# Cross-attention: the last of 257 keys is taken off all the others

## The reference

```python
q = hidden_states @ Wq
k = encoder_hidden_states @ Wk
v = encoder_hidden_states @ Wv
scores = einsum('bhsd,bhkd->bhsk', q, k) * scale
probs = softmax(scores, axis=-1)
out = einsum('bhsk,bhkd->bhsd', probs, v)      # then @ Wo + bo
```

## Time and profile before

| what | before |
|---|---|
| median of 3 runs | 1652.82 us (1651.26 to 1653.18) |
| profiled execution, its own time | 1654.9 us |
| its span, first to last instruction | 1653.0 us |
| mean granted TensorE clock | 0.988 |
| TensorE busy | 1592.7 us |
| VectorE / ScalarE / GpSimd busy | 1112.3 / 771.1 / 240.4 us |

### The profile page before, as it was taken

How to read it: one execution, slowest core, us unless ns; L and a number is a source line. 1 busy time by engine, 2 the same in 40 slices (tenths; PEclk the granted TensorE clock), 3 DMA queues, 4 the chain that set the end, 5 groups by cost and what they waited for, 6 DMA issues and landing times.

```text
span 1653.0 us, 33814 instructions
## 1 busy us (share of the span) xinstructions
PE 1592.7 (96%) x12498; PEld 1324.8 (80%) x12498; DVE 1112.3 (67%) x2350; ACT 771.1 (47%) x1683; POOL 240.4 (15%) x153
## 2 busy tenths in 40 slices
PE   7999879999999999999999999999999999997989
PEld 6888668899989899898998898787878778775444
DVE  7776666677566766676566766657656665566788
ACT  4555554565555554555555553433123222222755
POOL 0000123232222223232222222100000000000000
PEclk9999989999999999999999999999999999998999
DMA  6898842331333213331323123250221311323022
GB/s 230 322 358 341 315 164 106 117 126 33 114 117 117 79 67 117 117 117 40 116 110 125 61 84 109 78 186 27 83 78 33 109 47 39 114 101 156 0 102 102
DMA packets 70812, 200.76 MB, mean 121 GB/s; under 512 B 4752, under 2 KB 22608, under 8 KB 67920
## 3 DMA queue, kind: packets, MB, share of 16 engines
q1 hardware_dynamic: 70736, 199.68, 32.6%
HBM read 129.28 MB, written 70.39 MB: 121 GB/s over the span
## 4 chain that ended last, share of the span: by engine, by line
PE 83%; issue 6%; DVE 6%; DMA 3%; ACT 1%; SPq 0%; POOLq 0%; POOL 0%; DVEq 0%
PE psum_o L672 16%; PE psum_s L641 12%; PE psum_o L1350 6%; PE psum_q L1350 5%; PE psum_o L687 5%; PE psum_q L700 5%; PE psum_o L533 5%; PE psum_q L1390 4%; PE psum_q L641 4%; PE psum_t L1418 4%; PE psum_t L652 3%; PE psum_t L612 2%; PE psum_s L1404 2%; PE psum_q L659 2%; PE psum_s L1377 1%
## 5 line engine op out<-in xcount | busy, mean ns | idle before, releaser
L672 PE MATMUL psum_o<-pT,c_nat 128*128 128x512 f32 x1152 | 311.6, 407 | 4.7 <-issue 3.5
L641 PE MATMUL psum_s<-cT,qk 128*128 128x258 f32 x1728 | 254.1, 291 | 10.0 <-ACT probs L861 5.3
L641 PEld LDWEIGHTS psum_s<-cT,qk 128*128 128x128 f32 x1728 | 227.0, 191 | 21.4 <-issue 6.2
L672 PEld LDWEIGHTS psum_o<-pT,c_nat 128*128 128x128 f32 x1152 | 205.1, 191 | 41.3 <-DVE pT L926 4.5
L1208 POOL TENSOR_TENSOR c_nat<-c_raw,zero 128x768 fp32r<-128x768 f32 x64 | 95.3, 1490 | 799.7 <-PE psum_o L672 603.4
L861 ACT ACTIVATE probs<-psum_s,nmax 128x257 f32<-128x257 f32 x192 | 91.7, 478 | 222.9 <-DVE nmax L1112 222.7
L1096 DVE SCALAR_TENSOR_TENSOR oT<-p_last,c_last,psum_o 128x512 f32<-128x512 f32 x192 | 143.2, 746 | 69.8 <-PE psum_o L672 67.5
L926 DVE TENSOR_TENSOR pT<-psum_t,pT 128x512 fp32r<-128x512 f32 x128 | 87.8, 687 | 73.1 <-ACT pT L752 73.1
L1211 POOL TENSOR_TENSOR c_nat<-c_raw,c_nat 128x768 fp32r<-128x768 f32 x64 | 122.3, 1911 | 5.0
L752 ACT ACTIVATE cT<-psum_t 128x256 fp32r<-128x256 f32 x192 | 67.5, 389 | 113.8 <-PE psum_t L612 113.8
L1112 DVE TENSOR_REDUCE nmax<-psum_s 128x1 f32<-128x257 f32 x192 | 81.0, 422 | 50.4 <-PE psum_s L641 49.6
(11 more groups left out here) (268 smaller groups left out, 3022.8 us busy)
## 6 DMA issues: line engine op xcount, KB each, us to landing
qk_by_tile<-staged SPq DMA_DIRECT2D x32, 1536.0 KB, 9.9
raw<-qk_by_tile SPq DMA_DIRECT2D x16, 3072.0 KB, 9.9
c_raw<-in_ctx_dram SPq DMA_DIRECT2D x64, 384.0 KB, 3.2
out_dram<-x_out SPq DMA_DIRECT2D x32, 256.0 KB, 2.1
x_res<-in_x_dram SPq DMA_DIRECT2D x16, 256.0 KB, 2.7
x_in<-out_dram SPq DMA_DIRECT2D x4, 1024.0 KB, 7.9
x_res<-out_dram SPq DMA_DIRECT2D x16, 256.0 KB, 2.8
x_all<-out_dram SPq DMA_DIRECT2D x1, 4096.0 KB, 13.2
```

The lines of the kernel that those rows point to most:

```text
L641: m = pe.matmul(ps[:, 0:SKP], qk[:, part, rg, c, b, :], cT[b % 2][:, moving, c, :], start=(c, part, moving) == (0, 0, 0), stop=(c, part) = ...
L672: i = pe.matmul(ps[:], c_nat[(b - 1) % 2][:, part, k, m * P:(m + 1) * P], pT[:, moving, k, :], start=(k, part, moving) == (0, 0, 0), stop= ...
```

## The change

Softmax doesn't change when one number is added to all scores of a row. So GpSimd now subtracts the last context row from the other 256 (`c_raw` in place, `pool_less_last`). The 257th score is then always zero, and since the probabilities sum to one, the attended result only lacks the last context row itself. What follows in the code:

- `pe_probs_last`, `act_probs_last` and `act_last_key` go; `cT`'s column 256 is zeroed once for each buffer. The scores are still 258 columns wide. The scalings cover 256 columns in place of 257.
- `dve_attended` becomes one addition of a column (`c_last`) to what it reads from PSUM. `c_last` comes from `rem_all`, unsplit.
- The context's high part goes from GpSimd to ScalarE (`act_ctx_high`), in its list between the probabilities' high parts and the next `qk` piece or exp 1. It waits for the subtraction of the same batch. GpSimd's low part waits for it.
- GpSimd's list in turn `b` is: low part of batch `b`, then the subtraction for batch `b+1` (in the "first" section one for batch 0 stands ahead).
- `pe_ctxT` waits for that subtraction (`s_sub`) in place of the load.
- Each context load is followed by a second one, which spreads the last row over 128 partitions (`last_row`, 1536 bytes each).
- Scores 3 use bank q1 in place of s0.

```diff
@@ pe_ctxT
             if chunks[0] == 0:
-                pe.wait_ge(s_ctx[(b + 1) % 2], 32 * t + 16 * ((b + 1) // 2 + 1))
+                pe.wait_ge(s_sub, 4 * t + (b + 2))
@@ pe_cross_tile
                 pe_scores(pe, t, b, 2, section)
-                if before:
-                    pe_probs_last(pe, t, b, section)
@@ ScalarE
+        def act_ctx_high(act, t, b, section):
+            i = b % 2
...
+            act.wait_ge(s_sub, 4 * t + (b + 1))
+            nc.scalar.activation(flat(c_nat[i][:, 0, :, :]), flat(c_raw[i][:]), ACT.Copy).then_inc(s_chi, 1)
@@ act_cross_tile
                 if before:
                     for k in range(2):
                         act_probsT(act, t, b, k, section)
+                act_ctx_high(act, t, b, section)
                 if b == 3 and more:
                     act_qk_high(act, t + 1, 0)
                 exp(b, 1)
...
-                if before:
-                    act_probs_last(act, t, b, section)
...
-                    act_last_key(act, b + 1, 4 * t)
@@ dve_attended
-            nc.vector.scalar_tensor_tensor(oT[:, m, :, (b - 1) % 4, :], p_last[:].rearrange("p (s q) -> p s q", q=SQ),
-                                           c_last[:, (b - 1) % 2, m:m + 1], ps[:].rearrange("p (s q) -> p s q", q=SQ),
-                                           ALU.mult, ALU.add).then_inc(free, 1)
+            nc.vector.tensor_scalar(oT[:, m, :, (b - 1) % 4, :], ps[:].rearrange("p (s q) -> p s q", q=SQ),
+                                    c_last[:, (b - 1) % 2, m:m + 1], None, ALU.add).then_inc(free, 1)
@@ GpSimd
+        def pool_less_last(pool, t, b):
+            i = b % 2
+            pool.wait_ge(s_ctx[i], 64 * t + 32 * (b // 2 + 1))
+            row_ = last_row[i][:].rearrange("p (a d) -> p a d", a=1).to_broadcast([P, 2, DC])
+            nc.gpsimd.tensor_tensor(c_raw[i][:], c_raw[i][:], row_, ALU.subtract).then_inc(s_sub, 1)
@@ pool_split
-            G.tensor_tensor(flat(c_nat[i][:, 0, :, :]), flat(c_raw[i][:]), zero[:].to_broadcast([P, 2 * DC]),
-                            ALU.add).then_inc(s_chi, 1)
             pool.wait_ge(s_chi, 4 * t + (b + 1))
             G.tensor_tensor(c_nat[i][:, 1, :, :], c_raw[i][:], c_nat[i][:, 0, :, :].bitcast(F32),
                             ALU.subtract).then_inc(s_nat, 1)
@@ pool_cross_tile
+            if section == "first":
+                pool_less_last(pool, t, 0)
             for b in range(4):
                 pool_split(pool, t, b, section)
+                if section != "last" or b < 3:
+                    pool_less_last(pool, t, b + 1)
@@ load_ctx
+            last = keys[:, 2 * P:SK, :].rearrange("a k d -> (a k) d").to_broadcast([P, DC])
+            sp.dma_start(last_row[ahead % 2][:], last).then_inc(s_ctx[ahead % 2], 16)
```

More of the change, by code:

```diff
@@ L68, in cross_units @@
     for b in range(4):
-        u += [(("S", b, rg), ("s0", "s1", "q0", "s0")[rg]) for rg in range(4)]
+        u += [(("S", b, rg), ("s0", "s1", "q0", "q1")[rg]) for rg in range(4)]
         if b or section != "first":
@@ L87, in split_only @@
 def split_only(units):
-    return [u for u in units if u[0][0] in ("XT", "Q", "WK", "RT", "CT", "PT", "W")]
+    return [u for u in units if u[0][0] in ("XT", "Q", "WK", "CT", "PT", "W")]
 def split_only2(units):
@@ L278, in build_kernel @@
         c_raw0 = sb("c_raw0", [P, 2, DC], F32)
[L279 to L284, removed]
+        rem_all = nc.alloc_sbuf_tensor_at("rem_all", [P, KC, NB], F32, offset=X_BUFS + 2 * DC * 4)
+        last_row = [sb(f"last_row{i}", [P, DC], F32) for i in range(2)]
         c_raw1 = nc.alloc_sbuf_tensor_at("c_raw1", [P, 2, DC], F32, offset=X_BUFS)
@@ L630, in pe_scores @@
         def pe_scores(pe, t, b, rg, section):
-            if rg == 0:
-                pe.wait_ge(s_key, 4 * t + (b + 1))
+            if section == "first" and rg == 0 and b < 2:
+                pe.wait_ge(s_zero, b + 1)
             if b == 0:
@@ L653, in pe_probsT @@
                 m.then_inc(done, 1)
[L655 to L661, removed]
         def pe_pv(pe, t, b, m, section):
@@ L787, in act_start_weights @@
             if r:
-                act_high(act, project(("RT",)), flat(remT[:, 0, :, :]), cols(KC * NB))
+                ps, free = full(act, project(("RT",)))
+                nc.scalar.activation(flat(rem_all[:]), ps[:, 0:KC * NB], ACT.Copy).then_inc(free, 1)
         def act_qk_high(act, t, rg):
@@ L794, in act_qk_high, with act_last_scalars @@
                                  raw[:, :, rg, :].rearrange("p h (a q) -> p h a q", q=SQ), ACT.Copy).then_inc(s_qhi, 1)
[L796 to L804, removed]
+        def act_last_scalars(act, t, b, section):
+            if section == "first" and b == 0:
+                taken(act, project(("RT",)))
+            elif b == 0:
+                act.wait_ge(drained["o1"], U1.before("o1", t, section, 1))
+            elif section != "first" or b > 1:
+                taken(act, U1(("PV", b - 1, 2), t, section))
+            batch = 4 * t
+            later = rem_all[:, :, b:]
             one = later[:, :, batch:batch + 1] if isinstance(batch, int) else later[:, :, bass.ds(batch, 1)]
@@ L825, in act_project_all @@
                 else:
-                    act_last_key(act, 0, 0)
                     for c in range(KC):
@@ L838, in act_wo_high @@
             nc.scalar.activation(wo_high[:, 4 * h:4 * h + 4, :], wo_raw[:, 4 * h:4 * h + 4, :], ACT.Copy).then_inc(s_wohi, 1)
[L840 to L847, removed]
+        def act_ctx_high(act, t, b, section):
+            i = b % 2
+            if b > 1 or (b == 1 and section != "first"):
+                full(act, U1(("PV", b - 1, 2), t, section))
+            elif b == 1:
+                full(act, U1(("CT", 0, 2), t, section))
+            elif section == "first":
+                full(act, project(("CT", "start", 2)))
+            else:
+                act.wait_ge(filled["o1"], U1.before("o1", t, section))
+            act.wait_ge(s_sub, 4 * t + (b + 1))
+            nc.scalar.activation(flat(c_nat[i][:, 0, :, :]), flat(c_raw[i][:]), ACT.Copy).then_inc(s_chi, 1)
         def act_probsT(act, t, b, k, section):
@@ L893, in act_cross_tile @@
                 if after:
-                    act_last_key(act, b + 1, 4 * t)
                     ctxT(b, 0)
                     ctxT(b, 1)
-                if section == "first" and b == 0:
-                    act.wait_ge(s_remsum, 1)
-                act_last_scalars(act, b, 4 * t)
+                act_last_scalars(act, t, b, section)
                 if b == 3 and not more:
```

37 lines of the change are left out of this document (12 added, 25 removed).

## The result

| | before | changed |
|---|---|---|
| median | 1652.72 us | 1691.26 us (1691.20 to 1691.82, 4 runs) |
| ratio | | 1.0237, 95% interval 1.0224 to 1.0249 |
| profiled execution / its span | 1654.9 / 1653.0 us | 1691.8 / 1690.0 us |
| mean granted clock | 0.988 | 0.987 |

The account below looks back on a forecast made before the run. TensorE, busy 100.00 of 100 us in the loop, was taken to bound the kernel. Loop tiles (14 x 2.48 = 34.7) and edges (+4.0) added 38.7 to 1654.9, so 1693.6 profiled, 1691 us median; range 1672 to 1708.

Parts of the forecast that it names:

- TensorE saves 0.44 a turn: Every batch: the four turnings of the 257th probability leave TensorE, 0.44 us each time, 28.2 us over 64 batches.
- The chain delivers 1.20 late: Batches 1 and 3: TensorE waits 1.20 us for GpSimd's subtraction ahead of the context's turning, +0.76 a turn.
- The fourth batch: Fourth batch of a tile: VectorE's `qk` low part comes 1.57 us late, so the turn grows by 1.4 us.
- The sum: Whole kernel: 14 loop tiles of +2.48 give 34.7, with edges of +4.0 38.7; profiled 1693.6, median 1691 us.
- The first tile: First tile: subtraction (2.0) behind a late context load, some 2 us of queued loads, and the fourth batch: +5 us.
- the last tile and the tail: Last tile: +0.76 - 0.44 + 0.76 - 0.44, and -1.16 for a wait in its fourth batch; tail: -0.44.
- the -0.11 of the fourth batch: VectorE's chain in the fourth batch: two `dve_attended` fall from 746 ns to about 690, so -0.11 us.
- The faster rival: Every turn: the subtraction is hidden and only the 28.2 us saved show, 1625 us; chance 0.05.
- The clock rival: After each of 45 waits TensorE's clock halves for 3.3 us, losing 1.65 each: 74 us, 1765; chance 0.05.
- The lock the other way: Fourth batch: VectorE's `qk` low part starts before the subtraction, which waits for it; +2.1, 15 times: 1722; chance 0.05.
- The load: Context load issued 2.2 us later plus a second load: over 4 us of cover; rival of it late 1735, chance 0.02.

Follow-up runs that it names:

- the held variant: Changed kernel with the subtraction ahead of GpSimd's low part, but held until the last product of the turn before is done; 1644.41 us, ratio 0.9950.
- the second experiment: Changed kernel with GpSimd's subtraction for batch b+1 put ahead of the low part of batch b, not held; 1667.38 us, ratio 1.0084.

## Why the prediction was right

- **TensorE saves 0.44 a turn.** Right where the turn is TensorE's: the covered turn of batch 2 shrank by 0.47, and plain turns by 0.45 without the wait.
- **The chain delivers 1.20 late.** Measured 1.26 (11.28 against 10.02), +0.81 a turn where I had +0.76. Its pieces: high part 853 ns where I had 840, low part 1.85, subtraction 1.82 where I had taken 1.85 from the low part. The repeated operand costs GpSimd nothing.
- **The fourth batch.** +1.26 (0.81 in its own turn, 0.45 more stall in the next scores 0) where I had 1.4. The subtraction held VectorE back as the earlier trace rows had shown. I had its low part 1.57 late (0.84 for ScalarE's shift, the rest for the subtraction); the experiments give 0.72 and 0.73. By the rule of the Trainium skill, "SBUF — State Buffer", section "Who interferes with whom", a VectorE `tensor_tensor` with both inputs in SBUF and a GpSimd instruction that reads SBUF lock each other out whole, and order of arrival decides; the runs agree to 0.2 us, in both orders: 2.48 for VectorE behind the subtraction, 3.20 for a subtraction behind VectorE.
- **The sum.** A loop tile +2.40 against +2.48, 14 of them 33.6 against 34.7. The first tile: +4.25 by the third group of scores 0 of the second tile (251.95 against 247.70), where I had 5. What is left, 37.0 - 33.6 - 4.25 = -0.85, stands against my -1.0 for the last tile and the tail, but it isn't a reading of them: the rest of the second tile's first turn is in it with 0.6 more than in the loop, the last tile, from the third group of its first scores 0, and the tail are -0.7, and -0.7 comes behind the cross stage, where I had nothing. The terms add to 38.7, the spans differ by 37.0 and the medians by 38.5: the terms were good to some 2 us, and that the median came within 0.3 is partly luck.
- **A term I had wrong:** `dve_attended` without its product takes 747 ns, not 690. What costs is the column and not the third operand: in the kernel before, the same operation with a third tensor and a constant in place of the column takes 691. So the -0.11 of the fourth batch wasn't there; without it I would have had 1.5 against 1.26, and the two errors partly cancelled.

```profile
L1001 DVE SCALAR_TENSOR_TENSOR qT<-psum_o,qT 128x512 fp32r<-128x512 f32 x32 | 22.1, 691 | 48.3 <-ACT qT L769 48.1
```

- **The faster rival** was priced too well: hidden, the change brings some 21 us, not 28, since VectorE's chain keeps one turn in four from half of its gain, and the edges bring less; 23 were reached only by taking work off that chain. I knew that chain for the forecast and forgot it for the rival.
- **The clock rival** was rightly small for this kernel: waits of 1.03 us left the clock at 1.00 in the whole loop. It was near, though: waits of 1.77 us took it to about 0.6 in nine of 12 tiles. The 1.65 us that I had for one fall was a good size, 1.57 measured.
- **The lock the other way** did not come in this kernel: the subtraction began 0.97 us ahead of the `qk` low part (520.80 against 521.77) where I had 1.05, and none of the 64 took over 1.86 us. The kernel with two subtractions shows it.
- **The load** had cover: in the loop of the changed kernel no subtraction waited for it. Where one had to in the held variant, it started 5.45 us after the row's load was issued (580.89 against 575.44). The changed kernel issues that load at 566.07 and asks for it in the next turn, 5.9 us in (565.29 against 559.40), so at 570.68 + 5.9 = 576.6. By this estimate some 5 us of cover were left, where I had over 4.

## What to carry to other kernels

When one engine sets the time, price a new operation by where its inputs let it start, and not by how busy its engine is: GpSimd was idle for 70% of the loop, and one operation more on it cost nothing there when GpSimd's list could begin with the turn, but the same work cost 57 us more when its list had to begin behind a ScalarE copy, some 10 of them (14 x 0.72) because that copy also pushed back ScalarE's own work behind it. Before an operation is moved to a less busy engine, look at what that engine's list does first and who waits behind it there. And an operation that may start as soon as its data are there may start at the worst moment, as the subtraction at 519.63 did: hold it to one when the engine that it collides with is quiet.

## What I had not expected of the hardware

- A wait can cost TensorE more than its length, and the same wait doesn't always. Three waits a tile of 1.03 us: clock 1.00 behind all of them. One a tile of 1.77 us: 0.58 to 0.63 over the next 4.1 us in nine tiles of 12, and 1.00 in three. 2.92 us: 0.66 over the next 5 us in one place and 1.00 in another. 4.34 us: 0.50 to 0.63 over the next 4. A fall cost about 1.57 us of the turn. What decides between the two isn't shown.
- VectorE reading 512 columns from PSUM with one column added takes 747 ns, as with a multiply and a third tensor (746), where a plain copy takes 689 and a third tensor without a column 691. ScalarE does the same addition in 731 ns, where its plain copies take 591 to 600.
- VectorE's scalings of 256 columns in SBUF, which have one input there and not two, wait for a GpSimd operation as well (1.54 us for two instead of 0.60, in the second experiment).
